# Scan step of a test-time-training layer: the order of TensorE's products, and the place of one VectorE mask

## Reference, cut to what matters

```python
def step(carry, inp):
    W1c, b1c = carry
    xq, xk, xv, et = inp
    Z1 = xk @ W1c + b1c
    grad = _ln_fused_l2_bwd(Z1, xv - xk, gw, gb)
    Attn = jnp.tril(xq @ jnp.swapaxes(xk, -1, -2))
    b1_bar = b1c - jnp.tril(et) @ grad
    Z1_bar = xq @ W1c - et * Attn @ grad + b1_bar
    last_eta = et[:, :, -1, :, None]
    W1n = W1c - jnp.swapaxes(last_eta * xk, -1, -2) @ grad
    b1n = b1c - (last_eta * grad).sum(-2, keepdims=True)
    return ((W1n, b1n), xq + _ln(Z1_bar, gw, gb))
```

## Time and profile before

| | |
|---|---|
| median of 3 runs | 494.38 us (493.9 to 495.05) |
| profiled execution, its own time | 494.99 us |
| its span, first to last instruction | 493.2 us |
| busy over the span: PE, DVE, ACT, POOL | 82%, 62%, 60%, 40% |
| granted TensorE clock, mean | 0.915 |
| first and last gradient of the scan | 128.4 us and 259.0 us |

### The profile page before, as it was taken

The page is one execution under the profiler, slowest core; times in us unless marked ns, Lnnn a source line. Parts: engine busy times, 40 slices in busy tenths (PEclk is TensorE's granted clock), DMA queues, the critical chain, the costliest instruction groups (busy, mean ns, idle before and its releaser), DMA issues. The chain is left out here.

```text
span 493.2 us, 10289 instructions
## 1 busy us (share of the span) xinstructions
PE 404.1 (82%) x3168; PEld 268.1 (54%) x3168; DVE 307.6 (62%) x1068; ACT 293.9 (60%) x707; POOL 196.5 (40%) x279
## 2 busy tenths in 40 slices
PE   0799999997899999999991699983799365785991
PEld 0443443434677778777770477763353151665980
DVE  4664632703577777777771447777579996456096
ACT  1265756756376676667661446663578934596634
POOL 1001642802388888888873800004417670000003
PEclk9999999998899999999996559997799976997996
DMA  8110222224112222222213320000000001000002
GB/s 232 18 52 23 66 79 81 66 84 141 35 48 64 65 64 64 64 64 64 64 55 107 101 50 1 2 0 1 0 1 0 1 1 23 1 1 1 0 1 85
DMA packets 35164, 23.06 MB, mean 47 GB/s; under 512 B 10287, under 2 KB 34877, under 8 KB 35133
## 3 DMA queue, kind: packets, MB, share of 16 engines
q1 hardware_dynamic: 34716, 22.55, 17.0%
q10 hardware_dynamic: 416, 0.13, 0.1%
HBM read 13.20 MB, written 9.47 MB: 46 GB/s over the span
## 5 line engine op out<-in xcount | busy, mean ns | idle before, releaser
L451 PE MATMUL bank<-w,hT 128*128 128x385 f32 x128 | 48.5, 505 | 0.0
L903 ACT ACTIVATE win<-bank 128x384 f32<-128x384 f32 (+1 forms) x124 | 43.2, 399 | 0.1
L832 PE MATMUL bank<-win,wst 128*32 128x128 f32 x1024 | 42.5, 281 | 0.0
L451 PEld LDWEIGHTS bank<-w,hT 128*128 128x128 f32 x128 | 22.4, 189 | 30.2 <-issue 20.9
L1164 ACT ACTIVATE std_<-mv_,cst 128x2 f32<-128x2 f32 (+1 forms) x46 | 13.5, 296 | 36.6 <-DVE mv_ L1144 19.8
L1377 POOL TENSOR_TENSOR win<-win,lng 128x512 f32<-128x512 f32 x2 | 2.5, 1268 | 77.2 <-ACT win L1658 77.2
L832 PEld LDWEIGHTS bank<-win,wst 128*32 128x32 f32 x1024 | 25.2, 110 | 7.8 <-issue 0.2
L1393 PE MATMUL bank<-xn1T,w1e 128*128 128x512 f32 x32 | 17.7, 677 | 12.3 <-ACT he L1554 12.1
L970 POOL TENSOR_SCALAR xh<-raw,bmv,brs 128x128 f32<-128x128 f32 x32 | 25.5, 796 | 3.0 <-DVE brs L1022 2.9
L827 PE MATMUL bank<-win,cst 128*128 128x128 f32 x128 | 25.2, 279 | 0.7 <-DVE grad L1069 0.7
L963 POOL TENSOR_TENSOR xkm<-win,wst 128x256 f32<-128x256 f32 x32 | 19.7, 614 | 14.1 <-PE bank L849 12.1
(11 more groups left out here) (301 smaller groups left out, 1209.0 us busy)
## 6 DMA issues: line engine op xcount, KB each, us to landing
rows_scratch<-stage SPq DMA_DIRECT2D x32, 192.5 KB
win<-rows_scratch SPq DMA_DIRECT2D x32, 192.5 KB, 2.4
attn_scratch<-ob SPq DMA_DIRECT2D x32, 64.0 KB, 1.6
att<-attn_scratch SPq DMA_DIRECT2D x32, 64.0 KB
xt<-in_L_attn_x SPq DMA_DIRECT2D x4, 256.0 KB, 5.9
out<-win SPq DMA_DIRECT2D x4, 256.0 KB, 2.4
cst<-in_constants SPq DMA_DIRECT2D x1, 535.5 KB, 4.2
w<-in_L_attn_wk SPq DMA_DIRECT2D x2, 128.0 KB, 4.9
```

Of the source, the lines that this page charges most:

```text
L451: mm = nc.tensor.matmul(rows_bank(i, h)[:, 0:RC], hT[:, k, i * P:(i + 1) * P], w4[:, k, h, :], start=(k == 0), stop=(k == 1))
L832: mm = nc.tensor.matmul(dst[32 * b:32 * b + 32, 0:F], v[:, at:at + 2 * K], w_sb[:, state, first_slot(b) + h, :], start=False, stop=(h == 1 ...
L903: nc.scalar.activation(w_sb[:, state, at:at + n, :], bank[b][:, 0:n * F].rearrange("f (h g) -> f h g", h=n), ACT.Copy).then_inc(w_done, 1)
```

## The change

In the step, TensorE's products are put in another order. The bias product of `base` becomes a function of its own, `base_bias`. The output's bias product is issued right behind L845, ahead of the eight updates; the eight column-tile products of the output's base follow the eight row-tile updates directly; the gram products come after them. The bias product for z stands ahead of the transposes. On VectorE the pair mask is issued behind the sum over gy instead of ahead of it. No product is added or taken away.

```diff
+                def base_bias(dst, state, copied):
+
+                    if copied is not None:
+                        wait(pe, w_done, copied + 2)
+                    nc.tensor.matmul(dst[:, 0:F], con("ident"), w_sb[:, state, 2, :], start=True, stop=False,
+                                     skip_group_check=True)
+
                 def base(dst, v, state, copied):
 
                     for half in range(2):
                         if copied is not None:
                             wait(pe, w_done, copied + 2 * half + 2)
-                        if half == 0:
-                            nc.tensor.matmul(dst[:, 0:F], con("ident"), w_sb[:, state, 2, :], start=True, stop=False,
-                                             skip_group_check=True)
...
                         pe.wait_ge(xkm_done, t + 1)
                         nc.tensor.matmul(bank[0][:, 2 * F:3 * F], blkt[:], g_t, start=False, stop=False, skip_group_check=True)
+                    wait(pe, raw_done, t)
+                    base_bias(zbar_bank, p % 2, None if isinstance(t, int) and t == 0 else 4 * (t - 1))
+                    if left:
                         for h in range(H):
                             for b in range(B):
                                 own = slice(32 * b, 32 * b + 32)
...
+                    base(zbar_bank, queries(p), p % 2, None if isinstance(t, int) and t == 0 else 4 * (t - 1))
                     if left >= 2:
                         grams(t + 2, (p + 2) % RING)
-                    wait(pe, raw_done, t)
-                    base(zbar_bank, queries(p), p % 2, None if isinstance(t, int) and t == 0 else 4 * (t - 1))
                     pe.wait_ge(mask_done, t + 1)
                     nc.tensor.matmul(zbar_bank[:, 0:F], pm[:, p % 2, :], g_t, start=False, stop=True,
                                      skip_group_check=True).then_inc(zbar_mm, 1)
+                    if left >= 2:
+                        base_bias(zbanks[p % 2], (p + 1) % 2, 4 * t)
                     if left >= 3:
                         transposes(t + 3, (p + 3) % RING)
                     if left >= 2:
...
                     mark(nc.vector.tensor_scalar(r2[:], r[:], r[:, 0:1], 1.0 / F, ALU.mult, ALU.mult))
+                    need(gys)
+                    sums = mark(nc.vector.scalar_tensor_tensor(out=junk[:], in0=z, scalar=mean, in1=gy[:],
+                                                               op0=ALU.subtract, op1=ALU.mult, accum_out=es[:]))
                     if left and not (isinstance(s, int) and s == 0):
                         pair_mask(s, p)
-                    need(gys)
-                    need(mark(nc.vector.scalar_tensor_tensor(out=junk[:], in0=z, scalar=mean, in1=gy[:],
-                                                             op0=ALU.subtract, op1=ALU.mult, accum_out=es[:])))
+                    need(sums)
```

More of the change, by code:

```diff
@@ L877, in _ @@
                 transposes(1, 1)
+                base_bias(zbanks[0], 0, None)
                 base(zbanks[0], keys(0), 0, None).then_inc(z_mm, 1)
@@ L883, in _ @@
                 grams(1, 1)
+                base_bias(zbanks[1], 0, None)
                 base(zbanks[1], keys(1), 0, None)
```

## The result

Over six runs each, the changed kernel takes 499.06 us against 494.53 us before (medians). The measured ratio, which compares the means, is 1.0088 with a 95% interval of 1.0052 to 1.0124: slower by 2.6 to 6.1 us. The forecast was 497.8, slower by 3.4. Its runs spread from 495.97 to 500.87; those of before lie within 493.8 to 495.05 here, but over 29 later runs they spread as widely, 491.75 to 498.07.

The account below looks back on a forecast made before the run. TensorE's own order was taken to set the 4.20 us step; 0.22 saved by order and a 0.39 us stall at the transposes gave 4.33. Over the scan +3.4 us on the 494.38 median: 497.8 us, 8-in-10 range 493.8 to 501.5.

Parts of the forecast that it names:

- TensorE's order: In the scan's step, one whole-array visit between two tile groups goes; by order alone 4.20 becomes 3.98 us, saving 0.22.
- rival 2: At the row-to-column tile passage: no switch, grams 0.13 us earlier, step 4.20 us, kernel 494.2 us; chance 0.11.
- The grams' end and the mask: L817 starts 2.43 us behind L842 and ends at 2.82; the pair mask waits for it, 2.86 to 3.14.
- The release: From the pair mask's end through TensorE's sequencer to the transposes' load: 0.23 us, load at 3.37 instead of 2.98.
- The rest of the step: Behind the stalled load: second transpose at 3.54 us, 0.20 to the tiles, 0.58 to the end; step 4.33 us.
- The mask behind the sum: On VectorE, the moved pair mask would start at 2.86 us anyway: no effect on the stall, gradient's end at 3.66 hidden.
- The copies: ScalarE's state copies, needed by z's base, end at 3.24 us, even at 3.46 before the tiles at 3.74.
- The sum: Over the scan: 28 x 0.13 = 3.6 us, step 29 -0.2, steps 30 and 31 nothing; together +3.4 us.
- the multiplication by 28: Transposes are issued in 29 of 32 steps, 28 counted as the first has other waits; 0.13 us each, 3.6 us.

Follow-up runs that it names:

- the transposes last and the copies together: Changed kernel with the two transposes behind z's base and ScalarE's four state copies ahead of the scaled gy; 0.9853 of the kernel before, 487.55 us.
- Release on the load: Changed kernel with implied transpose waits left out, the rows' wait ahead of z's bias, the pair mask's on the weight load; 0.9956 of the kernel before.

## Why the prediction was right

- **TensorE's order, -0.22 us.** Right, and right about the passage between the two kinds of tiles: 0.66 us from the start of L856 to the start of L836 (203.37 to 204.03), the full price and no discount, so rival 2 falls. The Trainium skill (TensorEngine Tiling (Array Packing), Key Properties) says that a change of the tiling mode drains TensorE. The 0.66 us agrees with it, though the trace shows only the time. What the order is worth once nothing waits is seen with the transposes last and the copies together: 3.96 in three steps of four and 4.00 in the mean, against 4.20. The forecast's own order, transposes ahead of z's base, was never run without a wait; its nearest is 4.16, with the release at 0.05.
- **The grams' end and the mask.** Forecast 2.43 for L817 and 2.86 for the mask behind the start of L846; measured 2.44 and 2.86.
- **The release, 0.23 us.** Measured 0.23 from the mask's end to the load (205.65 to 205.88), inside bounds of 0.18 and 0.38. The runs split it in three: 0.11 for the second wait instruction, 0.07 for the first (0.12 to 0.05), and 0.05 left when the load itself carries the wait. The forecast had 0.15 and 0.08, and the 0.08 came from a place where the array was not idle as the text says: the column tiles ahead of that load run to 164.02. So the sum is right and the split was not, and that 0.23 came out to the hundredth is in part luck.
- **The rest of the step.** Second transpose forecast at 3.54, measured 3.54; tiles 3.74 and 3.75; step 4.33 and 4.34. PE is busy for 96.8% of the steady part, forecast some 95%. The weight loads stand idle for 0.30 us ahead of L808, forecast 0.4.
- **The mask behind the sum.** No effect, as forecast. But the working had VectorE free for the mask at 2.69. The sum starts at 2.24 and not 2.30, and an operation that does not need it can follow 0.27 us later and not 0.39, the distance of one that does; so it is 2.51. In the changed kernel the wait for the grams hides the slip; the expectation for the mask's move alone was wrong by it.
- **The copies.** The text had them end at 3.24, or up to 3.46 if they moved with the updates; in the changed kernel they end at 3.21 to 3.25, ahead of the tiles, as forecast. They cost something only with the transposes last, 0.14 to 0.16 us a step, where z's base starts at 3.10 and not at the 3.40 that the text set against them.
- **The sum.** 3.4 us forecast, 4.5 between the medians, with an interval of 2.6 to 6.1 us. The scan grew by 2.3 us in the first profile and 3.6 in the second; the low clock at its head, present in the profile before, was absent in the first of them. The second is the one to compare, and there the multiplication by 28 holds. The last distance between gradients fell by 0.38 us (3.79 to 3.41) where the sum had 0.2. The rest of the difference is inside the interval.

Left open: the changed order with no wait for the mask at all. The transposes write the same PSUM bank that VectorE reads for the mask, so a wait keeps the two in order; the Trainium skill asks for such a guard (PSUM — Partial Sum Buffer, PSUM bank collisions raise a hardware error), and no run here shows what happens without it. Release on the load is the nearest to it that was run. Also open is what sets the places of the low clock, by which executions of one kernel differ by some 1%.

## What to carry to other kernels

When an engine's order is rearranged to save switches, follow each group that moves later to the semaphore it raises, through the other engine, and back to the instruction here that waits for it: a product moved 0.8 us later cost more than the switch it saved. A wait that shows nowhere in a profile may be hidden by a tenth of a microsecond or two; in the step of the earlier trace rows this one had a margin of 0.16 us (the mask's end at 208.53 plus 0.23, against a load at 208.92). And put the wait that really ends last on the instruction that needs it, with implied waits left out: 0.23 us from release to start became 0.05.

## What the runs showed of the hardware that was not expected

A wait that is already satisfied cost 0.11 us where TensorE's sequencer met it behind one that was not (0.23 us from the mask's end to the load, 0.12 without it), and 0.05 us is left when the load itself carries the only wait. On VectorE an operation that does not need the sum starts 0.27 us behind an instruction with an accumulated result, one that does 0.39 us. In the scan a switch from row tiles straight to column tiles costs as much as one to the whole array: 0.66 us from the start of the row tiles to what follows them, against 0.65. Two executions of the same kernel had their stretches at the low clock at other places: behind the scan the clock came back some 5 us later in one profile than in the other, and the work between two fixed points took 2.1 us longer there.
